# Queries and keys of two heads from seven block products instead of eight, in the QKV block of a transformer kernel

## The chip, the cores and the metric

The kernel runs on one core of one Trainium2 chip. A core has TensorE (PE: matmuls, and PEld, the loading of their weights), VectorE (DVE), ScalarE (ACT), GpSimd (POOL) and SyncE (SP, which here only issues DMAs). They run side by side, each through its own list of instructions in a fixed order, and wait for one another by semaphores that the code sets by hand. The metric is the time of one execution on the device, in microseconds (us), as the median of several runs.

## The reference, cut to what matters

x is 1024 tokens of 512 numbers in fp32; the kernel computes six residual layers, of which the change touches the second:

```python
x = x + 0.5 * ffn(layernorm(x), ...)
x = x + attn(layernorm(x), Wq, bq, Wk, bk, Wv, bv, Wo, bo, gq, gk)   # 32 heads of 128
x = x + 0.5 * ffn(layernorm(x), ...)
x = x + 0.5 * ternary_ffn(x, ...)
x = x + retrieval_attn(layernorm(x), ...)
x = x + 0.5 * ternary_ffn(x, ...)

def attn(h, ...):
    q = rms_norm(h @ Wq + bq, gq)     # over all 4096 numbers of a token
    k = rms_norm(h @ Wk + bk, gk)
    v = h @ Wv + bv
    # softmax(q k^T / sqrt(128)) v, head by head, then @ Wo + bo
```

## The kernel before

Stages: a feed-forward layer to 93 us, the layer norm's tail to 101, **the QKV block from 101.4 to 638.4**, attention to 1740, then the rest. Matmuls are made in pairs of parts: each fp32 operand is split into a high part (fp32r, written by ACT) and a low part, the rest (by DVE, or POOL), and a product is high x high + high x low + low x high, three matmuls of 128x128 by 128x512 for every 128 of the 512 inputs (`product`, printed as L402 in the profile). So one unit, a tile of 128 outputs by 512 tokens, is 4 x 3 = 12 matmuls into one bank of PSUM.

The QKV block works in eight groups of four heads (`groups`: the first and last are written out, those between are a loop). A group has three phases, Q, K and V, of eight units each (u // 2 is the head, u % 2 the half of the tokens; for V a unit is 128 tokens by four heads). Its 1 MB of weights for a phase is loaded as one tile, split by ACT in one instruction (L734, 128x2048) and by DVE in one (`split`, L767), a whole phase before PE needs it. Per unit: DVE evicts the bank with the bias added (L826, or L824 for V) into one of four `res` tiles; for a query ACT writes the high part scaled with the gain (L752) and DVE the low part (`q_low`, L801), which SP stores to a scratch tensor in DRAM; keys and values are stored from `res` as they are. For the later RMS norm ACT squares every query and key tile (L755, `sq`, two buffers) and POOL adds the square to an accumulator (L865). In the first group POOL also adds the output bias to x (L855, eight times).

PE's only waits in the loop are for the phase's low weights (`w_lo_done`) and for the bank of four units ago (`res_done`). `ln_xT_hi`/`ln_xT_lo` are the two parts of x^T, normalised and transposed. The layer norm writes them at the end of the feed-forward stage, a 128-token tile at a time (L326 on ACT: high part; DVE: low part), and PE computes the first two units of the first phase, the queries, between its transposes.

## Time and profile before

| | |
|---|---|
| median of 3 runs | 2321.61 us (2321.32 to 2323.63) |
| the profiled execution's own time | 2324.25 us |
| its span | 2322.5 us |
| mean granted clock of TensorE in it | 0.989 |
| PE busy | 2256.0 us, 97% of the span |
| DVE busy | 1609.4 us, 69% |
| ACT busy | 1135.6 us, 49% |
| POOL busy | 828.8 us, 36% |

Rows of groups read: line of the code, engine, operation, output<-inputs, partitions x elements and types, x count, then busy us and mean ns of one, then idle time of the engine before them and what ended it. Rows of a timeline read: start us, duration us, engine, line, operation, output<-inputs; in brackets the idle time before it and who ended it. Durations of matmuls overlap, so the distance of two starts is what one costs; in a run of one instruction on DVE or ACT the next also starts slightly before the reported end of the last. Tile names are those of the program's buffers, some of which serve several purposes.

### The profile page before, as it was taken

The numbers are of one execution on the slowest core, as the hardware profiler recorded it, in microseconds if no ns is written. First come the engines' busy times: TensorE is split into PE (matmuls) and PEld (weight loads), VectorE is DVE, ScalarE is ACT, GpSimd is POOL, SyncE is SP. The second block draws the span as 40 slices with busy tenths as digits, with TensorE's granted clock in tenths as the row PEclk, the third lists the DMA queues.
The fourth block names the chain that finished last, engine by engine and source line by source line (L and its number), as shares of the span: only waits on it lengthen the run. The fifth ranks groups of instructions, "written<-read, shape, count | busy, mean of one in ns | idle before, by whom it ended". The sixth has DMA issues, their size and how long they took to land. (4 is left out here: it accounts for less than half of the span.)

```text
span 2322.5 us, 34366 instructions
## 1 busy us (share of the span) xinstructions
PE 2256.0 (97%) x11044; PEld 1874.1 (81%) x11044; DVE 1609.4 (69%) x2654; ACT 1135.6 (49%) x1845; POOL 828.8 (36%) x736
## 2 busy tenths in 40 slices
PE   7899999999989999999999999999998999899998
PEld 5688888888778888888888888888886788687887
DVE  5544444444378888888888888888886665785765
ACT  3233332322266666666666666666663344352442
POOL 4553332233222222212212222222214466672565
PEclk9999999999999999999999999999999999999999
DMA  3155555455332211211221221221201111141210
GB/s 114 47 181 191 190 177 183 168 187 184 132 107 71 81 55 67 81 66 56 81 72 50 81 72 50 81 78 44 81 24 41 51 68 44 33 129 37 73 59 37
DMA packets 106182, 210.47 MB, mean 91 GB/s; under 512 B 9728, under 2 KB 42496, under 8 KB 102784
## 3 DMA queue, kind: packets, MB, share of 16 engines
q1 hardware_dynamic: 106112, 209.57, 26.9%
q8 instruction: 39, 0.64, 0.1%
q14 instruction: 31, 0.25, 0.0%
HBM read 140.33 MB, written 69.21 MB: 90 GB/s over the span
## 5 line engine op out<-in xcount | busy, mean ns | idle before, releaser
L1106 ACT ACTIVATE at_pT_hi<-ps 128x512 fp32r<-128x512 f32 x512 | 278.3, 595 | 352.3 <-PE ps L1210 352.2
L1148 DVE TENSOR_REDUCE at_small<-ps 128x1 f32<-128x1024 f32 x256 | 312.5, 1221 | 84.0 <-PE ps L402 83.0
L1158 DVE TENSOR_TENSOR at_pT_lo<-ps,at_pT_hi 128x512 fp32r<-128x512 f32 x512 | 327.1, 680 | 3.8 <-ACT at_pT_hi L1106 3.8
L1113 ACT ACTIVATE at_probs<-ps,at_small,cols 128x1024 f32<-128x1024 f32 x256 | 309.2, 1208 | 28.2 <-DVE at_small L1150 21.6
L865 POOL TENSOR_TENSOR qkv_acc<-qkv_acc,qkv_sq 128x512 f32<-128x512 f32 x128 | 166.2, 1299 | 320.1 <-ACT qkv_sq L755 316.5
L1210 PEld LDWEIGHTS ps<-ident,at_probs 128*128 128x128 f32 x2048 | 239.2, 140 | 37.9 <-issue 4.4
L1210 PE MATMUL ps<-ident,at_probs 128*128 128x128 f32 x2048 | 266.4, 273 | 3.2 <-DVE at_pT_lo L1158 3.2
L1172 DVE SCALAR_TENSOR_TENSOR x<-ps,at_small,x 128x512 f32<-128x512 f32 x256 | 192.0, 750 | 10.2 <-PE ps L402 3.1
L1043 POOL TENSOR_TENSOR at_o_lo<-at_o_raw,at_o_hi 128x512 fp32r<-128x512 f32 x32 | 41.2, 1288 | 439.8 <-ACT at_o_hi L1127 439.8
L402 PE MATMUL ps<-ln_xT_hi,ln_xT_lo 128*128 128x512 f32 x768 | 196.0, 390 | 0.0
L826 DVE TENSOR_SCALAR qkv_res<-ps,cols 128x512 f32<-128x512 f32 x128 | 94.9, 748 | 141.7 <-PE ps L402 122.7
L1235 PE MATMUL ps<-at_pT_hi,ln_xT_lo 128*128 128x512 f32 x512 | 180.6, 393 | 0.7 <-DVE at_y_lo L1144 0.7
L402 PEld LDWEIGHTS ps<-ln_xT_hi,ln_xT_lo 128*128 128x128 f32 x768 | 144.2, 188 | 30.7
L402 PE MATMUL ps<-ln_xT_hi,q_hi 128*128 128x512 f32 x480 | 148.0, 390 | 0.0
L752 ACT ACTIVATE qkv_q_hi<-qkv_res,cols 128x512 fp32r<-128x512 f32 x64 | 46.3, 723 | 194.6 <-DVE qkv_res L826 194.6
L755 ACT ACTIVATE qkv_sq<-qkv_res 128x512 f32<-128x512 f32 x128 | 80.0, 625 | 121.3 <-DVE qkv_res L826 104.8
L402 PE MATMUL ps<-at_o_hi,at_y_hi 128*128 128x512 f32 x256 | 122.0, 477 | 3.9 <-DVE x L1172 3.5
L402 PE MATMUL ps<-ln_xT_hi,first_hi 128*128 128x512 f32 x280 | 113.3, 405 | 7.1 <-DVE ln_xT_lo L282 4.0
L1043 POOL TENSOR_TENSOR ln_xT_hi<-kn,ln_xT_hi 128x1024 fp32r<-128x1024 f32 x31 | 74.2, 2393 | 116.0 <-ACT ln_xT_hi L1083 116.0
L1235 PEld LDWEIGHTS ps<-at_pT_hi,ln_xT_lo 128*128 128x128 f32 x512 | 96.0, 188 | 22.1 <-issue 0.9
L824 DVE TENSOR_TENSOR qkv_res<-ps,qkv_bv 128x512 f32<-128x512 f32 x64 | 43.5, 688 | 98.9 <-PE ps L402 98.8
L402 PE MATMUL ps<-ln_xT_hi,first_lo 128*128 128x512 f32 x280 | 111.1, 397 | 0.0
(273 smaller groups left out, 5636.4 us busy)
## 6 DMA issues: line engine op xcount, KB each, us to landing
scratch_q_hi<-qkv_q_hi SPq DMA_DIRECT2D x64, 256.0 KB, 2.1
scratch_q_lo<-qkv_q_lo SPq DMA_DIRECT2D x64, 256.0 KB, 2.3
scratch_k<-qkv_res SPq DMA_DIRECT2D x64, 256.0 KB, 2.8
scratch_v<-qkv_res SPq DMA_DIRECT2D x64, 256.0 KB, 2.3
k_raw<-scratch_k SPq DMA_DIRECT2D x32, 512.0 KB, 3.8
at_v_raw<-scratch_v SPq DMA_DIRECT2D x32, 512.0 KB, 3.3
wq_raw<-in_Wq SPq DMA_DIRECT2D x8, 1024.0 KB, 6.5
qkv_w<-in_Wk SPq DMA_DIRECT2D x8, 1024.0 KB, 5.0
```

The source lines that it names most:

```text
L402: last = nc.tensor.matmul(out, s, m, start=(start and n == 0), stop=(stop and n == len(terms) - 1))
L755: nc.scalar.activation(sq[:, u % 2, :], res[u % 4][:], ACT.Square).then_inc(sq_done, 1)
L826: nc.vector.tensor_scalar(res[u % 4][:], core.bank(u % 4), bias[t][:, bass.ds(g * GROUP + u // 2, 1)], None, ALU.add)\
L865: nc.gpsimd.tensor_tensor(part, part, sq[:, u % 2, :], ALU.add).then_inc(acc_done, 1)
L1043: nc.gpsimd.tensor_tensor(dst, a, b, ALU.subtract).then_inc(done, 1)
L1106: nc.scalar.activation(pT2[jp][0][:, 4 * b:4 * b + 4, w * P:(w + 1) * P], T_BANKS[:, b * HALF:(b + 1) * HALF].rearrange("p (k n) -> p k n" ...
L1113: nc.scalar.activation(probs[l % 4][:], scores(l)[:], ACT.Exp, bias=nbias[:, l % 4:l % 4 + 1], scale=rq[:, l % NT:l % NT + 1], accum_out=s ...
L1148: nc.vector.reduce_max(maxes[:, l % 4:l % 4 + 1], scores(l)[:], AX.X).then_inc(s_max, 1)
L1158: nc.vector.tensor_tensor(pT2[jp][1][out], T_BANKS[:, b * HALF:(b + 1) * HALF].rearrange("p (k n) -> p k n", k=4), pT2[jp][0][out], ALU.su ...
L1172: nc.vector.scalar_tensor_tensor(out=x[:, tile, :], in0=core.bank(WO_BANK), scalar=rsums[:, c:c + 1], in1=x[:, tile, :], op0=ALU.mult, op1 ...
L1210: last = nc.tensor.transpose(T_BANKS[:, k * P:(k + 1) * P], probs[(l - T_LAG) % 4][:, k * P:(k + 1) * P], core.ident[:])
L1235: last = nc.tensor.matmul(core.bank(PV_BANK), a[:, k, :], b[:, k, :], start=(c == 0 and n == 0), stop=(c == 3 and n == len(terms) - 1))
```

## The change

Queries and keys are no longer made unit by unit, but in **quads**: one quad is the queries, or the keys, of two heads, that is four units (two heads by two halves of the tokens, 512 each), as a 2x2 block product of the weights' blocks A11, A12, A21, A22 (inputs 0 to 255 or 256 to 511 by head 1 or 2) and the blocks of x^T B11, B12, B21, B22. A group has four quads: j = 0 queries, 1 keys, 2 queries, 3 keys, and c = 4g + j counts them. The 2x2 product is made in the form of Strassen and Winograd, from seven products P1 to P7 of six matmuls each in place of eight, with four sums of weight blocks S1 to S4 per quad, four sums T1 to T4 of x^T made once, and sums of products:

```
P1 = A11 B11   P2 = A12 B21   P3 = S4 B22   P4 = A22 T4   P5 = S1 T1   P6 = S2 T2   P7 = S3 T3
U2 = P1 + P6   U3 = U2 + P7
C11 = P1 + P2   C21 = U3 + P4   C22 = U3 + P5   C12 = U2 + P5 + P3
```

P1, P6, P7 and P4 are added up in one PSUM bank (`e_bank`), which is read after each of the first three: `keep_p1` (ACT, into a tile printed as rk), `keep_u2` (DVE, qkv_u), `keep_u3` (ACT, qkv_u). P5 and P3 share a second bank, P2 has a third. The weight sums are made by POOL (`sums_of_weights`), their high parts by ACT (`high`, instructions of 512, 768, 256 and 256 columns), their low parts by DVE (`low`, the same sizes), a quad ahead of their use; C21 is evicted by ACT, the other three by DVE. P4 and P3 of quad j-1 are issued after P1 of quad j.

The rest: the weights of a quad are loaded as 512 KB; the value weights are split in four pieces of 128x512, two in step 0 and two in step 2 of the next group, instead of in one; the eight units of values of a group stand after its four quads, with P4 and P3 of quad 3 behind the first; in the first group six of the eight units come first, of which two lie between the transposes of the layer norm, where two query units lay; the layer norm also keeps x^T in fp32 (two ACT copies of 128x2x128 per tile), from which DVE makes T1 to T4 (four instructions of 128x2x512), ACT their high parts and DVE and POOL two low parts each.

The diff, cut to its core:

```diff
+        if self.keep is not None:
+            for t in [k - 4] if k < self.STEPS - 1 else [NT - 2, NT - 1]:
+                if t >= 0:
+                    act.wait_ge(self.s_lo, t + 1)
+                    for i, part in enumerate(self.keep):
+                        last = self.nc.scalar.activation(part[:, :, t * P:(t + 1) * P],
+                                                         self._psum(t)[:, 2 * i:2 * i + 2, :], ACT.Copy)
+                    last.then_inc(self.s_kept, 1)
...
-            wait(pe, self.s_lo, t - 1)
+            wait(pe, self.s_lo if self.keep is None else self.s_kept, t - 1)
...
+            def sums_of_weights(g, j):
+                c, w = g * QUADS + j, raw[j % 2]
+                s = [s_raw[:, i, :].rearrange("p (k c) -> p k c", k=2) for i in range(4)]
+                a11, a12, a21, a22 = w[:, 0:2, 0, :], w[:, 2:4, 0, :], w[:, 0:2, 1, :], w[:, 2:4, 1, :]
+                pool.wait_ge(w_in[j % 2], nth(g, j) * 16 + 16)
+                wait(pool, late_lo, c)
+                nc.gpsimd.tensor_tensor(s[0], a21, a22, ALU.add).then_inc(s_made, 1)
+                nc.gpsimd.tensor_tensor(s[2], a11, a21, ALU.subtract).then_inc(s_made, 1)
+                pool.wait_ge(s_made, c * 4 + 1)
+                nc.gpsimd.tensor_tensor(s[1], s[0], a11, ALU.subtract).then_inc(s_made, 1)
+                pool.wait_ge(s_made, c * 4 + 3)
+                nc.gpsimd.tensor_tensor(s[3], a12, s[1], ALU.subtract).then_inc(s_made, 1)
+            def add_square(g, j, kind):
+                m = (g * QUADS + j) * 4 + kind
+                pool.wait_ge(sq_done, m + 1)
+                pool.wait_ge(acc_done, m + 2)
+                part = acc[j % 2][:, half(kind) * HALF:(half(kind) + 1) * HALF]
+                nc.gpsimd.tensor_tensor(part, part, sq[:, kind % 2, :], ALU.add).then_inc(acc_done, 1)
...
+                for j in range(QUADS):
+                    if j + 1 < QUADS:
+                        sums_of_weights(g, j + 1)
+                    if j > 0:
+                        for kind in (C22, C21, C12):
+                            add_square(g, j - 1, kind)
+                    add_square(g, j, C11)
+                    if is_first(g):
+                        add_output_bias(j)
+                if not is_last(g):
+                    sums_of_weights(g + 1, 0)
+                for kind in (C22, C21, C12):
+                    add_square(g, QUADS - 1, kind)
+                if is_last(g):
...
+            def high(g, j):
+                c, w, o = g * QUADS + j, raw[j % 2], left_hi[j % 2]
+                act.wait_ge(w_in[j % 2], nth(g, j) * 16 + 16)
+                wait(act, p7_done, c - 1)
+                nc.scalar.activation(o[:, 0:2 * PART].rearrange("p (k c) -> p k c", k=KB), w[:, :, 0, :], ACT.Copy)\
+                    .then_inc(left_hi_done, 1)
+                act.wait_ge(s_made, c * 4 + 3)
+                nc.scalar.activation(o[:, S1 * PART:(S3 + 1) * PART].rearrange("p (s n) -> p s n", s=3),
+                                     s_raw[:, 0:3, :], ACT.Copy).then_inc(left_hi_done, 1)
+                wait(act, p3_done, c - 1)
+                nc.scalar.activation(o[:, A22 * PART:(A22 + 1) * PART].rearrange("p (k c) -> p k c", k=2),
+                                     w[:, 2:4, 1, :], ACT.Copy).then_inc(left_hi_done, 1)
+                act.wait_ge(s_made, c * 4 + 4)
+                nc.scalar.activation(o[:, S4 * PART:(S4 + 1) * PART], s_raw[:, 3, :], ACT.Copy)\
+                    .then_inc(left_hi_done, 1)
+            def shared(g, j, kind):
+                n, m = nth(g, j), (g * QUADS + j) * 4 + kind
+                act.wait_ge(c_done[kind], g * QUADS + j + 1)
+                if is_query(j):
+                    wait(act, q_stored[kind], n * 32)
+                    nc.scalar.activation(q_hi[kind][:], res[kind][:], ACT.Copy,
+                                         scale=gain_now[:, head(j, kind):head(j, kind) + 1]).then_inc(q_hi_done, 1)
+                wait(act, acc_done, m + 1)
+                nc.scalar.activation(sq[:, kind % 2, :], res[kind][:], ACT.Square).then_inc(sq_done, 1)
...
+            def keep_p1(g, j):
+                c = g * QUADS + j
+                act.wait_ge(p1_done, c + 1)
+                wait(act, c_done[C11], c)
+                nc.scalar.activation(p1, e_bank(j), ACT.Identity, bias=bias(j, C11)).then_inc(p1_kept, 1)
+            def keep_u3(g, j):
+                c = g * QUADS + j
+                act.wait_ge(p7_done, c + 1)
+                wait(act, c_done[C22], c)
+                nc.scalar.activation(u3, e_bank(j), ACT.Identity, bias=bias(j, C22)).then_inc(u3_kept, 1)
+            def evict21(g, j):
+                c = g * QUADS + j
+                act.wait_ge(p4_done, c + 1)
+                res_free(act, g, j, C21)
+                nc.scalar.activation(res[C21][:], e_bank(j), ACT.Identity, bias=bias(j, C21)).then_inc(c_done[C21], 1)
...
+                act.wait_ge(now_done, g + 1)
+                for j in range(QUADS):
+                    keep_p1(g, j)
+                    if j > 0:
+                        shared(g, j - 1, C22)
+                        evict21(g, j - 1)
+                        shared(g, j - 1, C21)
+                        shared(g, j - 1, C12)
+                    if j + 1 < QUADS:
+                        high(g, j + 1)
+                    if not is_first(g) and is_query(j):
+                        split_values(g, j)
+                        split_values(g, j + 1)
+                    shared(g, j, C11)
+                    keep_u3(g, j)
+                shared(g, QUADS - 1, C22)
+                evict21(g, QUADS - 1)
+                shared(g, QUADS - 1, C21)
+                shared(g, QUADS - 1, C12)
+                if not is_last(g):
+                    high(g + 1, 0)
 
             groups(act, body)
...
+            def low(g, j):
+                c, w, hi, lo = g * QUADS + j, raw[j % 2], left_hi[j % 2], left_lo[j % 2]
+                def piece(n, a, b, src, k):
+                    v.wait_ge(left_hi_done, c * 4 + n)
+                    return nc.vector.tensor_tensor(lo[:, a * PART:b * PART].rearrange("p (k n) -> p k n", k=k), src,
+                                                   hi[:, a * PART:b * PART].rearrange("p (k n) -> p k n", k=k),
+                                                   ALU.subtract)
+                wait(v, p7_done, c - 1)
+                piece(1, A11, S1, w[:, :, 0, :], KB)
+                piece(2, S1, A22, s_raw[:, 0:3, :], 3).then_inc(early_lo, 1)
+                wait(v, p3_done, c - 1)
+                piece(3, A22, S4, w[:, 2:4, 1, :], 2)
+                piece(4, S4, 7, s_raw[:, 3:4, :], 1).then_inc(late_lo, 1)
...
+            def evict(g, j, kind, bank, kept):
+                res_free(v, g, j, kind)
+                nc.vector.tensor_tensor(res[kind][:], bank, kept, ALU.add).then_inc(c_done[kind], 1)
+            def evict11(g, j):
+                c = g * QUADS + j
+                v.wait_ge(p2_done, c + 1)
+                v.wait_ge(p1_kept, c + 1)
+                evict(g, j, C11, A_BANK, p1)
+            def evict22(g, j):
+                c = g * QUADS + j
+                v.wait_ge(p5_done, c + 1)
+                v.wait_ge(u3_kept, c + 1)
+                evict(g, j, C22, d_bank(j), u3)
+            def keep_u2(g, j):
+                c = g * QUADS + j
+                v.wait_ge(p6_done, c + 1)
+                wait(v, c_done[C12], c)
+                nc.vector.tensor_scalar(u2, e_bank(j), bias_now[j % 2][:, head(j, C12):head(j, C12) + 1], None,
+                                        ALU.add).then_inc(u2_kept, 1)
...
+                for j in range(QUADS):
+                    if j > 0:
+                        evict22(g, j - 1)
+                        q_low(g, j - 1, C11)
+                        q_low(g, j - 1, C22)
+                        evict12(g, j - 1)
+                    keep_u2(g, j)
+                    if j > 0:
+                        q_low(g, j - 1, C21)
+                    if j + 1 < QUADS:
+                        low(g, j + 1)
+                    if j > 0:
+                        q_low(g, j - 1, C12)
+                    if not is_first(g) and is_query(j):
+                        split_values(g, j)
+                        split_values(g, j + 1)
+                    evict11(g, j)
+                evict22(g, QUADS - 1)
+                evict_values(g, units[0])
+                evict12(g, QUADS - 1)
+                if not is_last(g):
+                    v.wait_ge(c_done[C21], g * QUADS + QUADS)
+                    next_columns(g + 1)
+                    low(g + 1, 0)
+                for u in units[1:]:
+                    evict_values(g, u)
...
+            def times(out, j, part, right, more=False):
+                return product(nc, out, [(left(j, part, k), right[k]) for k in range(2)], start=not more, more=more)
+            def fourth(g, j):
+                c = g * QUADS + j
+                pe.wait_ge(u3_kept, c + 1)
+                pe.wait_ge(late_lo, c + 1)
+                times(e_bank(j), j, A22, T4, more=True).then_inc(p4_done, 1)
+            def third(g, j):
+                c = g * QUADS + j
+                pe.wait_ge(c_done[C22], c + 1)
+                times(d_bank(j), j, S4, B22, more=True).then_inc(p3_done, 1)
+            def second(g, j):
+                wait(pe, c_done[C11], g * QUADS + j)
+                times(A_BANK, j, A12, B21).then_inc(p2_done, 1)
...
+            def body(g):
+                for j in range(QUADS):
+                    c = g * QUADS + j
+                    pe.wait_ge(early_lo, c + 1)
+                    wait(pe, c_done[C21], c - 1)
+                    times(e_bank(j), j, A11, B11).then_inc(p1_done, 1)
+                    if j > 0:
+                        fourth(g, j - 1)
+                        third(g, j - 1)
+                    else:
+                        second(g, j)
+                    pe.wait_ge(p1_kept, c + 1)
+                    times(e_bank(j), j, S2, T2, more=True).then_inc(p6_done, 1)
+                    if j > 0:
+                        second(g, j)
+                    wait(pe, c_done[C12], c - 1)
+                    times(d_bank(j), j, S1, T1).then_inc(p5_done, 1)
+                    pe.wait_ge(u2_kept, c + 1)
+                    times(e_bank(j), j, S3, T3, more=True).then_inc(p7_done, 1)
+                for u in tail_units(g):
+                    values_unit(g, u)
+                    if u == tail_units(g)[0]:
+                        fourth(g, QUADS - 1)
+                        third(g, QUADS - 1)
```

**ScalarE, inside a group.** Before, at the end of a Q phase and in the K phase (qkv_w, wq: weight tiles):

```order
L752 ACTIVATE qkv_q_hi<-qkv_res,cols 128x512
L755 ACTIVATE qkv_sq<-qkv_res 128x512
L734 ACTIVATE qkv_w_hi<-qkv_w 128x2048
L755 ACTIVATE qkv_sq<-qkv_res 128x512 x8
L734 ACTIVATE wq_hi<-wq_raw 128x2048
```

After, step j = 1 of the first group, from `keep_p1(1)` to `keep_u3(1)` (ln_xn is the buffer of the squares, qkv_left_hi the high parts of quads 0 and 2, first_raw their weights, qkv_s_raw the sums):

```order
L930 ACTIVATE rk<-ps,cols 128x512
L918 ACTIVATE qkv_q_hi<-qkv_res,cols 128x512
L921 ACTIVATE ln_xn<-qkv_res 128x512
L942 ACTIVATE qkv_res<-ps,cols 128x512
L918 ACTIVATE qkv_q_hi<-qkv_res,cols 128x512
L921 ACTIVATE ln_xn<-qkv_res 128x512
L918 ACTIVATE qkv_q_hi<-qkv_res,cols 128x512
L921 ACTIVATE ln_xn<-qkv_res 128x512
L899 ACTIVATE qkv_left_hi<-first_raw 128x512
L902 ACTIVATE qkv_left_hi<-qkv_s_raw 128x768
L905 ACTIVATE qkv_left_hi<-first_raw 128x256
L908 ACTIVATE qkv_left_hi<-qkv_s_raw 128x256
```

Behind these stand the square of C11 (L921) and `keep_u3(1)` (L936). The one split of a phase became four pieces inside every step, between the copies that PE waits for.

**VectorE, inside a group.** Before, at the end of a Q phase and in the K phase:

```order
L826 TENSOR_SCALAR qkv_res<-ps,cols 128x512
L801 SCALAR_TENSOR_TENSOR qkv_q_lo<-qkv_res,cols,qkv_q_hi 128x512
L767 TENSOR_TENSOR qkv_w_lo<-qkv_w,qkv_w_hi 128x2048
L826 TENSOR_SCALAR qkv_res<-ps,cols 128x512
L801 SCALAR_TENSOR_TENSOR qkv_q_lo<-qkv_res,cols,qkv_q_hi 128x512
L826 TENSOR_SCALAR qkv_res<-ps,cols 128x512 x7
```

After, step j = 1 of the first group (L1016 evicts C22, C12 of quad 0 and last C11 of quad 1, L1040 is `keep_u2(1)`, L992 `low(2)`):

```order
L1016 TENSOR_TENSOR qkv_res<-ps,qkv_u 128x512
L1009 SCALAR_TENSOR_TENSOR qkv_q_lo<-qkv_res,cols,qkv_q_hi 128x512 x2
L1016 TENSOR_TENSOR qkv_res<-ps,qkv_u 128x512
L1040 TENSOR_SCALAR qkv_u<-ps,cols 128x512
L1009 SCALAR_TENSOR_TENSOR qkv_q_lo<-qkv_res,cols,qkv_q_hi 128x512
L992 TENSOR_TENSOR qkv_left_lo<-first_raw,qkv_left_hi 128x512
L992 TENSOR_TENSOR qkv_left_lo<-qkv_s_raw,qkv_left_hi 128x768
L992 TENSOR_TENSOR qkv_left_lo<-first_raw,qkv_left_hi 128x256
L992 TENSOR_TENSOR qkv_left_lo<-qkv_s_raw,qkv_left_hi 128x256
L1009 SCALAR_TENSOR_TENSOR qkv_q_lo<-qkv_res,cols,qkv_q_hi 128x512
L1016 TENSOR_TENSOR qkv_res<-ps,rk 128x512
```

The four low parts now stand between `keep_u2(1)` and the eviction of C11 of the same quad.

**GpSimd, the first group.** Before:

```order
L850 MEMSET qkv_acc 128x1024 x2
L855 TENSOR_TENSOR x<-x,qkv_bo 128x512 x8
L865 TENSOR_TENSOR qkv_acc<-qkv_acc,qkv_sq 128x512 x16
```

After, one step (second_raw is the weights of quads 1 and 3, acc the accumulator, rk the output bias here):

```order
L840 TENSOR_TENSOR qkv_s_raw<-second_raw 128x256
L841 TENSOR_TENSOR qkv_s_raw<-second_raw 128x256
L843 TENSOR_TENSOR qkv_s_raw<-qkv_s_raw,second_raw 128x256
L845 TENSOR_TENSOR qkv_s_raw<-second_raw,qkv_s_raw 128x256
L852 TENSOR_TENSOR acc<-acc,ln_xn 128x512 x4
L856 TENSOR_TENSOR x<-x,rk 128x512
```

Four weight sums came in ahead of every four additions.

## Rows read from the trace of the kernel before

**Rows 1.** The page's first part: busy time, share of the span, instructions, by engine

```profile
PE 2256.0 (97%) x11044; PEld 1874.1 (81%) x11044; DVE 1609.4 (69%) x2654; ACT 1135.6 (49%) x1845; POOL 828.8 (36%) x736
```

**Rows 2.** Window of a group: busy us (instructions) of PE, PEld, DVE, ACT, POOL; clock, DMA, GB/s

```profile
222.00:287.00 65.00, 65.00 (x289) 53.82 (x288) 29.40 (x37) 20.29 (x27) 20.63 (x16) 1.00 0.55 182
```

**Rows 3.** Timeline, PE at a unit's end, and the eviction of that unit

```profile
225.75 0.39 PE L402 MATMUL ps<-qkv_w_hi,ln_xT_lo 128*128 128x512 f32 x1
...
226.27 0.69 DVE L824 TENSOR_TENSOR qkv_res<-ps,qkv_bv 128x512 f32<-128x512 f32 x1 [2.03 <-PE ps L402]
```

**Rows 4.** Timeline, DVE and ACT near the block's start, and DVE in a later group

```profile
110.52 3.00 DVE L767 TENSOR_TENSOR qkv_w_lo<-qkv_w,qkv_w_hi 128x2048 fp32r<-128x2048 f32 x1 [5.39 <-ACT qkv_w_hi L734]
113.44 1.40 DVE L826 TENSOR_SCALAR qkv_res<-ps,cols 128x512 f32<-128x512 f32 x2
...
117.02 1.11 DVE L801 SCALAR_TENSOR_TENSOR qkv_q_lo<-qkv_res,cols,qkv_q_hi 128x512 fp32r<-128x512 f32 x1
...
114.22 0.72 ACT L752 ACTIVATE qkv_q_hi<-qkv_res,cols 128x512 fp32r<-128x512 f32 x1 [3.72 <-DVE qkv_res L826]
114.84 0.61 ACT L755 ACTIVATE qkv_sq<-qkv_res 128x512 f32<-128x512 f32 x1
115.36 0.70 ACT L752 ACTIVATE qkv_q_hi<-qkv_res,cols 128x512 fp32r<-128x512 f32 x1
...
197.50 2.29 DVE L767 TENSOR_TENSOR qkv_w_lo<-qkv_w,qkv_w_hi 128x2048 fp32r<-128x2048 f32 x1 [2.46 <-ACT qkv_w_hi L734]
199.71 0.75 DVE L826 TENSOR_SCALAR qkv_res<-ps,cols 128x512 f32<-128x512 f32 x1
200.37 0.74 DVE L801 SCALAR_TENSOR_TENSOR qkv_q_lo<-qkv_res,cols,qkv_q_hi 128x512 fp32r<-128x512 f32 x1
```

**Rows 5.** A group of instructions, 93 to 645 us: busy us, mean ns | idle before

```profile
L841 DVE TENSOR_TENSOR kn<-k_raw,rk 128x1024 f32<-128x1024 f32 x1 | 1.2, 1226 | 0.1
```

**Rows 6.** ACT, all of line 1620: min/median/max ns, first and last start

```profile
L1620 ACT ACTIVATE rt_r<-ps,ln_small x16: 667/670/673, 2025.1 to 2095.6; 128x512 f32<-128x512 f32 x16
```

**Rows 7.** POOL: a timeline at 201 us, and groups or lines of its additions

```profile
201.36 4.04 POOL L865 TENSOR_TENSOR qkv_acc<-qkv_acc,qkv_sq 128x512 f32<-128x512 f32 x3 [4.24 <-ACT qkv_sq L755]
...
L865 POOL TENSOR_TENSOR qkv_acc<-qkv_acc,qkv_sq 128x512 f32<-128x512 f32 x128 | 166.2, 1299 | 320.1 <-ACT qkv_sq L755 316.5
L855 POOL TENSOR_TENSOR x<-x,qkv_bo 128x512 f32<-128x512 f32 x8 | 13.4, 1704 | 6.3 <-DMA qkv_bo<-in_bo 6.3
...
L1048 POOL TENSOR_TENSOR kn<-k_raw,rk x31: 2382/2409/2420, 647.3 to 1668.9; 128x1024 f32<-128x1024 f32 x31
```

**Rows 8.** DVE line 1678, the retrieval stage's low parts beside POOL

```profile
L1678 DVE TENSOR_TENSOR rt_wo_lo<-rt_wo,rt_wo_hi x8: 679/1364/1367, 2039.4 to 2111.1; 128x512 fp32r<-128x512 f32 x8
```

**Rows 9.** PE after two waits elsewhere (timeline), and windows behind them, columns as rows 2

```profile
640.23 0.47 PE L402 MATMUL ps<-first_hi,q_hi 128*128 128x512 f32 x1 [1.87 <-PEq L624]
640.54 0.39 PE L402 MATMUL ps<-first_lo,q_hi 128*128 128x512 f32 x1
...
2111.81 0.50 PE L402 MATMUL ps<-rt_wo_hi,rt_ret_hi 128*128 128x512 f32 x1 [2.06 <-DVE rt_wo_lo L1678]
...
641.00:650.00 9.00, 6.40 (x30) 4.53 (x28) 4.44 (x8) 4.29 (x7) 2.69 (x2) 1.00 0.78 262
2113.00:2117.00 4.00, 4.00 (x14) 3.09 (x13) 1.67 (x3) 2.32 (x3) 0.72 (x1) 0.57 0.00 0
```

**Rows 10.** The block's start on PE, and two loads (KB, us to landing)

```profile
114.24 0.80 PE L402 MATMUL ps<-ln_xT_hi,wq_hi 128*128 128x512 f32 x1 [6.94 <-DVE qkv_res L826]
...
115.26 0.63 PE L402 MATMUL ps<-ln_xT_hi,wq_lo 128*128 128x512 f32 x1
115.68 0.63 PE L402 MATMUL ps<-ln_xT_hi,wq_hi 128*128 128x512 f32 x1
...
qkv_w<-in_Wk SPq DMA_DIRECT2D x8, 1024.0 KB, 5.0
qkv_bv<-in_bv SPq DMA_DIRECT2D x8, 256.0 KB, 5.5
```

495 lines of the change are left out of this document (288 added, 207 removed).

## The prediction

> **What bounds the kernel now.** I read the page first. TensorE (PE) is busy for 2,256.0 of 2,322.5 us, VectorE (DVE) for 69% of it, ScalarE (ACT) for 49%, GpSimd (POOL) for 36% [rows 1]: PE sets the end. Then the window of one of the eight groups of heads, the block that changes. In 65.0 us PE is busy for 65.00 us and starts 289 matmuls, at full clock, so 288 distances: one starts every 0.226 us (0.2267 over the whole block). A group (3 projections x 8 units x 12 = 288 matmuls) takes 65.3 us. DVE has 29.4 us of work there, ACT 20.3, POOL 20.6 [rows 2]. There is no wait to win inside a group: the change can gain only by fewer matmuls, and loses where PE begins to wait for the other three.
>
> **What is removed.** A quad (queries or keys of two heads) takes seven products of six matmuls, 42, in place of 48. Four quads a group: 24 matmuls x 0.2267 us = 5.44 us a group, 192 matmuls and 43.5 us in all. Nothing else runs on PE in those slots, so all of it counts.
>
> **What is added on PE's path.** Before, PE waited only for a PSUM bank freed long ago. Now four products of a quad go into one bank, which is read in between: P1 is kept (ACT), P6 is added and the sum kept (DVE, `keep_u2`), P7 is added and kept (ACT, `keep_u3`), and P4 is added only then. Between P6(j) and P4(j) PE has work of its own: P6, P5, P7 and P1(j+1) for j = 0, which is 24 x 0.2267 = 5.44 us; P2 lies there too for j = 1 and 2, 6.80 us; for j = 3 a unit of values as well. Against that stands a chain which the order on the two engines fixes: `keep_u2(j)`, one low part of a query (where j-1 is a query), the four low parts of the next quad's weights, another query low part or the two low parts of value weights, `evict11(j)` on DVE; then on ACT the high part (of a query), the square, and `keep_u3(j)`. The durations:
> - a unit's last matmul starts at 225.75 and its eviction at 226.27, 0.52 later [rows 3]; from the start of P6 to `keep_u2` are five spacings, 0.52 and 0.05 for the semaphore (113.44 + 0.75 to 114.22 [rows 4]): 1.70 us.
> - PSUM evictions on DVE last 0.75 (with a bias column) and 0.69 (with a second operand), a query low part 0.74 [rows 3, 4], and the next starts some 0.09 before the reported end: 0.66, 0.60, 0.65.
> - a subtraction of two SBUF tiles lasts 1.23 us for 1,024 columns and 2.29 for 2,048 [rows 4, 5]: 1.04 per 1,024 and 0.16 fixed. The four low parts (512, 768, 256, 256 columns) follow one another in 0.61 + 0.88 + 0.35 + 0.35 = 2.19 us; two value low parts in 1.22.
> - ACT: after a square the next starts 0.52 later, after a query high part of 0.72 it is 0.62 [rows 4]; an eviction lasts 0.67 [rows 6], and I take 0.69 for `keep_u3`, which adds a bias column.
>
> Two more hand-overs are 0.10. For j = 0 the chain is 1.70 + 0.66 + 2.19 + 1.22 + 0.69 + 0.62 + 0.52 + 0.69 + 0.10 = 8.39 us against 5.44: PE waits 2.95. For j = 1 (a key: no high part; two query low parts): 1.70 + 0.66 + 0.65 + 2.19 + 0.65 + 0.69 + 0.52 + 0.69 + 0.10 = 7.85 against 6.80: 1.05. For j = 2: 8.39 against 6.80: 1.59. For j = 3 no weights stand in between: none. Together 5.59 us a group, already more than the 5.44 gained; over eight groups 44.7, less 2.4 in group 0, which has no value splits in these steps. **Bare: -43.5 + 44.7 - 2.4 = -1.2 us.**
>
> **What lengthens the chain.** POOL: a step gives it four sums of 128x256 and four squares of 128x512. Squares follow 1.35 us apart (4.04 for three; mean 1.30 alone), 1,024 columns take 2.41 [rows 7], so 256 columns take some 0.74, 0.79 with its semaphore. The ACT square of unit m waits until POOL has added m-2, and POOL has the next quad's four sums (3.1 us) ahead of three of its additions. Followed through, instruction by instruction, ACT's last square before the next high parts comes 1.24 us later than DVE is ready for it at j = 2, and 0.24 at j = 1: 1.5 us a group.
> Contention: two-input DVE work on SBUF is slower while POOL works. Beside POOL's `x += bo` (mean 1,704 ns against 1,299 for the same size) a low part of 2,048 took 3.00 us instead of 2.29, a query low part 1.11 instead of 0.74; the retrieval stage's 512-column low part took 0.68 at least, 1.36 in the middle [rows 4, 7, 8]. That is 0.36 us for each POOL instruction met, if the long one met two. Some five are met inside the three chains: 1.8 us a group. Bounds: 0, and twice that (the 1.36 row: 0.68 each). I take the first because it comes from this block's own instructions.
> A matmul after a wait is followed 0.31 us later, not 0.23 [rows 9]: 0.08 for each of some four waits, 0.3. Sum 3.6 a group, **+28.8 us**; bounds +2.6 (restarts only) and +43.
> The Trainium skill, "SBUF — State Buffer", section "Who interferes with whom", says that a DVE instruction with two SBUF inputs contends with a GpSimd instruction that reads SBUF and that the shared ports are an exclusive lock. If that meant one whole POOL instruction for each meeting, it would be nearer the 0.68; the 3.00 us row speaks for a part of one.
>
> **Clock.** A wait of 2.06 us was followed by a stretch at a granted clock of 0.57, one of 1.87 by 1.00 [rows 9]; 0.57 over 4 us is some 1.7 us lost. After the 6.94 us wait at 114.24 they start 0.43 apart [rows 10]: the lower of the two levels, 1.2 GHz. The waits at j = 0 and 2 (above 3 with contention and POOL's order) are longer than the 2.06 that was followed by a fall, that at j = 1 is shorter than the 1.87 that was not. Eight would be 13.6 us, sixteen 27, none 0; six falls, **+10 us**, because PE stays busy between the waits here more than in the retrieval stage.
>
> **Start and layer norm.** Before, the block starts with the 6.94 us wait for the value weights and a slow stretch of some 5 us behind it, matmuls 0.43 apart [rows 10]. After, values come first, from four pieces, and the first quad waits for the four sums of x^T (two-input subtractions of 1,024 columns, 1.23 each), for their low parts (two on POOL, 2.4 each) and for POOL's weight sums behind them; the bias of the values lands 5.5 us after its issue [rows 10]. I see waits of 2 to 4 and of some 3.5 us in place of 6.94 and the slow stretch: 0, bounds -5 and +6. In the layer norm's tail ACT makes two more copies per tile, which the next transposes wait for: **+1**, bounds 0 and 3 (256 columns are half of the 0.61 of 512 [rows 4]: two copies more for each of eight tiles, of which I count the last ones, where PE has little else). The end of the block changes little: the last values are still stored last; 0, bounds -2 and +3. On SP's queue the load for quad j+2 now stands ahead of the stores of quad j-1, and waits for the low parts of quad j; these are made a step earlier, so neither is held up, and 512 KB have a whole quad, 9.5 us, to land, where 1,024 KB land in 5.0 us [rows 10]: nothing.
>
> **Sum:** -1.2 + 28.8 + 10 + 1 = +38.6 against the profiled execution's own 2,324.25, so 2,362.9; that execution lay 2.6 above the median of its runs, 2,321.61, so I forecast a median of **2,360 us**.
>
> **Rivals.**
> A, the saving stays (faster). Mechanism: DVE and ACT finish their chain within PE's own work, so P4 never waits. For it: all three engines have spare time over a group (DVE 29.4 of 65.0). Against it: spare time doesn't help in a fixed order of which each piece waits for P6. Every us off the chain counts in three steps of eight groups, 24 us; the kernel becomes faster from a chain some 1.8 us shorter than with all additions above. Hidden but for 0.5 us a group: -43.5 + 4 + 1 gives 2,283. 8%.
> B, the bare chain is right, POOL costs little and the clock stays up: -1.2 + 2.6 + 1 gives 2,324, with the 1.5 us of POOL's order a group 2,336; from 2,318 to 2,340. For it: no row shows 256-column POOL work beside DVE. 15%.
> C, contention as in the 1.36 us row (1.6 a group more, +12.8) and a fall of the clock at both long waits (+17): 2,390, from 2,382 to 2,405. 17%. With the contention alone, the lock of the skill's page, it is 2,373, inside my main case.
> Main case, 2,340 to 2,382: 60%.
>
> **How the numbers follow.** The forecast is the main case's. 80% lie in 2,330 to 2,398: it leaves out A (8%), half of B and the far end of C. About 0.2%, 4.6 us, is what a measurement of this kernel can tell from no change. Faster by more: A and the fastest of B, 9%. Within it: the bare sum with nothing on top, 5%. Slower: 86%.
>
> **What would show it.** In the profile after: 10,852 matmuls; a window of one group some 69 us long in place of 65.3, and 70 with its fall of the clock; PE waits before P4 of quads 0, 1 and 2 released by `keep_u3`, some 3.2, 1.5 and 3.4 us with contention and POOL's order, none of quad 3; the low parts of 512 columns 0.69 us alone and about 1.05 beside POOL; ACT idle before a square on account of POOL's additions once or twice a group; granted clock below 1 after the j = 0 wait in most groups. Groups of 65 us or less would prove me wrong at the chain; waits of the right number but of 1 to 2 us, at the contention and POOL terms; full clock throughout, at the clock term. A first quad that waits for 10 us would be the start.

## The result, and the profile after

The changed kernel takes 2382.74 us (median of 4 runs, 2381.41 to 2382.99), against 2322.62 for the kernel before: 1.0252 times as long, 95% interval 1.0236 to 1.0268. The forecast was slower, at 2,360 us in a range of 2,330 to 2,398; 57 to 60 us were lost, where 38.6 had been added up. The profiled execution took 2381.41 us, span 2379.6, 57.16 us above the one of before. (Ahead of the forecast the kernel before had three runs, median 2321.61; a fourth, of 2329.48, moved the median to 2322.62.)

The page's first part, columns as in [rows 1]; TensorE has 192 matmuls less and is busy for 13 us less, all others have more:

```profile
PE 2242.9 (94%) x10852; PEld 1846.5 (78%) x10852; DVE 1686.6 (71%) x2794; ACT 1236.0 (52%) x2094; POOL 936.8 (39%) x865
```

The window of about one group, columns as in [rows 2]; and below it four microseconds behind or around the end of each of three waits of group 3 (groups are counted from 0):

```profile
300.00:372.00 72.00, 62.86 (x266) 50.30 (x265) 39.04 (x53) 32.11 (x57) 34.83 (x33) 0.98 0.50 165
336.00:340.00 4.00, 4.00 (x19) 3.29 (x19) 3.39 (x5) 3.40 (x6) 3.92 (x5) 1.00 0.57 166
348.00:352.00 4.00, 3.84 (x17) 3.18 (x18) 1.38 (x2) 2.65 (x5) 3.92 (x6) 1.00 0.82 291
362.00:366.00 4.00, 4.00 (x14) 3.11 (x14) 1.90 (x4) 2.64 (x6) 1.67 (x2) 0.70 0.53 160
```

266 matmuls now take 72 us, where 288 took 65.3. The timeline of TensorE's waits in that group (P4 of quad 0; P1 of quad 2, P4 of quad 1; P1 of quad 3, P4 of quad 2), and the same wait for P4 of quad 0 one group on:

```profile
334.79 0.50 PE L417 MATMUL ps<-qkv_right_hi,qkv_left_hi 128*128 128x512 f32 x1 [2.63 <-ACT qkv_u L936]
...
344.91 0.50 PE L417 MATMUL ps<-ln_xT_hi,qkv_left_hi 128*128 128x512 f32 x1 [1.68 <-DVE qkv_left_lo L992]
348.16 0.50 PE L417 MATMUL ps<-qkv_right_hi,queries 128*128 128x512 f32 x1 [1.60 <-ACT qkv_u L936]
357.12 0.50 PE L417 MATMUL ps<-ln_xT_hi,queries 128*128 128x512 f32 x1 [0.50 <-DVE first_parts L992]
361.53 0.79 PE L417 MATMUL ps<-qkv_right_hi,qkv_left_hi 128*128 128x512 f32 x1 [2.73 <-ACT qkv_u L936]
362.12 0.63 PE L417 MATMUL ps<-qkv_right_lo,qkv_left_hi 128*128 128x512 f32 x1
362.55 0.63 PE L417 MATMUL ps<-qkv_right_hi,qkv_left_lo 128*128 128x512 f32 x1
...
406.62 0.50 PE L417 MATMUL ps<-qkv_right_hi,qkv_left_hi 128*128 128x512 f32 x1 [2.63 <-ACT qkv_u L936]
```

The reader is to see three things. `keep_u3` (L936) releases three of the five waits, low parts (L992) the two others. A group takes 406.62 - 334.79 = 71.8 us. And the first 2.63 us wait is followed by matmuls at full clock (granted clock 1.00), the 2.73 us one by matmuls 0.43 apart (0.70 in its four microseconds), the lower level, called half clock below.

Why P1 of quad 2 waits is seen on the three other engines just before (timeline of step 1; DVE, ACT, POOL):

```profile
339.20 0.75 DVE L1040 TENSOR_SCALAR qkv_u<-ps,cols 128x512 f32<-128x512 f32 x1 [0.61 <-PE ps L417]
339.87 1.34 DVE L1009 SCALAR_TENSOR_TENSOR qkv_q_lo<-qkv_res,cols,qkv_q_hi 128x512 fp32r<-128x512 f32 x1
341.87 1.04 DVE L992 TENSOR_TENSOR qkv_left_lo<-first_raw,qkv_left_hi 128x512 fp32r<-128x512 f32 x1 [0.67 <-ACT qkv_left_hi L899]
342.84 2.02 DVE L992 TENSOR_TENSOR qkv_left_lo<-qkv_s_raw,qkv_left_hi 128x768 fp32r<-128x768 f32 x1
...
340.69 0.63 ACT L921 ACTIVATE ln_xn<-qkv_res 128x512 f32<-128x512 f32 x1 [1.26 <-POOL acc L852]
341.23 0.61 ACT L899 ACTIVATE qkv_left_hi<-first_raw 128x512 fp32r<-128x512 f32 x1
...
334.32 1.28 POOL L852 TENSOR_TENSOR acc<-acc,ln_xn 128x512 f32<-128x512 f32 x1 [21.05 <-ACT ln_xn L921]
335.55 0.73 POOL L840 TENSOR_TENSOR qkv_s_raw<-first_raw 128x256 f32<-128x256 f32 x1
...
339.36 4.68 POOL L852 TENSOR_TENSOR acc<-acc,ln_xn 128x512 f32<-128x512 f32 x3
```

POOL waits 21.05 us for a square, then makes four sums before its three additions; ScalarE waits for the additions with a square; its high part (L899), and with it DVE's low part, comes behind (DVE idles 0.67 us). The low part of 768 columns then takes 2.02 us; alone it is 0.955 (below). What made it longer is POOL's third addition, seen singly (timeline):

```profile
342.44 1.60 POOL L852 TENSOR_TENSOR acc<-acc,ln_xn 128x512 f32<-128x512 f32 x1
```

It runs to 344.04. The low part starts at 342.84, 1.20 us before that, and lasts 1.07 us longer than alone: it stands until the addition has ended, but for some 0.14 us. The addition in turn had started inside the low part of 512 columns (to 342.91) and lasts 0.31 us longer than alone. This holds throughout: in the loop (185 to 610 us) of the changed kernel 168 instructions of DVE have two SBUF inputs. 58 began while a POOL instruction ran and took as much longer as that one still had to run, less 0.14 us, each within 0.06 us (0.59 on average); the other 110 lasted as alone. Of POOL's 192 instructions there, 43 began inside such a DVE instruction and were longer by its rest, again less 0.14, each within 0.03 us; the other 149 lasted as alone. So a meeting has no fixed price: whoever comes second waits for the rest of the first.

The block from its first matmul behind the layer norm to attention's first takes 538.6 us before and 593.7 after; attention and all behind it are as long as before (1682.2 and 1682.1). The same count for every run, in us, from its profiled execution ("half clock" is what matmuls 0.43 apart cost over 0.2267 each, good to about 1 us). The profiled execution is one of the runs and not always near the median: no_pool's took 2342.3 us, u3_first's 2344.6, spread_start_c11's 2315.3.

| | median of runs | ratio to before | block | PE's waits | half clock |
|---|---|---|---|---|---|
| before | 2322.6 | | 538.6 | 9.7 | 5.1 |
| after | 2382.7 | 1.0252 | 593.7 | 79.0 | 22.4 |
| no_pool | 2334.7 | 1.0039 | 553.3 | 45.1 | 21.0 |
| no_squares_added | 2352.7 | 1.0109 | 565.7 | 51.2 | 26.3 |
| no_weight_sums | 2343.7 | 1.0096 | 553.4 | 56.5 | 7.5 |
| p1_repeated | 2370.9 | 1.0199 | 583.2 | 30.9 | 6.1 |
| c11_before_values | 2355.1 | 1.0132 | 564.9 | 64.8 | 8.5 |
| u3_first | 2348.9 | 1.0107 | 555.8 | 47.5 | 19.2 |
| sums_early_only | 2349.8 | 1.0115 | 561.8 | 64.3 | 7.9 |
| u3_first_sums_early | 2322.2 | 0.9992 | 532.2 | 34.0 | 10.1 |
| u3_sums_values_spread | 2319.7 | 0.9982 | 529.1 | 31.7 | 9.0 |
| spread_start_sums | 2316.6 | 0.9968 | 528.5 | 32.1 | 7.5 |
| spread_start_c11 | 2319.6 | 0.9978 | 527.0 | 29.6 | 8.8 |

### The profile page after: what moved, and what is told of

Its sections match the earlier page's. It is cut to its first block and busy times, and to the rows that moved or that the text cites. A ratio compares the mean times of both kernels' runs of the same rounds, so it can differ in the third digit from the quotient of the medians.

```text
span 2379.6 us, 34723 instructions
## 1 busy us (share of the span) xinstructions
PE 2242.9 (94%) x10852; PEld 1846.5 (78%) x10852; DVE 1686.6 (71%) x2794; ACT 1236.0 (52%) x2094; POOL 936.8 (39%) x865
## 5 line engine op out<-in xcount | busy, mean ns | idle before, releaser
L852 POOL TENSOR_TENSOR acc<-acc,ln_xn 128x512 f32<-128x512 f32 x128 | 177.3, 1385 | 255.0 <-ACT ln_xn L921 250.2
L417 PE MATMUL ps<-ln_xT_hi,queries 128*128 128x512 f32 x816 | 222.2, 392 | 8.2 <-DVE first_parts L992 8.2
L417 PE MATMUL ps<-ln_xT_hi,first_parts 128*128 128x512 f32 x656 | 221.4, 399 | 7.0 <-DVE ln_xT_lo L288 4.0
L417 PEld LDWEIGHTS ps<-ln_xT_hi,queries 128*128 128x128 f32 x816 | 153.2, 188 | 44.3 <-DVE first_parts L992 12.0
L417 PEld LDWEIGHTS ps<-ln_xT_hi,first_parts 128*128 128x128 f32 x656 | 125.5, 191 | 35.8 <-issue 4.8
L921 ACT ACTIVATE ln_xn<-qkv_res 128x512 f32<-128x512 f32 x128 | 79.9, 624 | 96.2 <-DVE qkv_res L1016 71.0
L1016 DVE TENSOR_TENSOR qkv_res<-ps,qkv_u 128x512 f32<-128x512 f32 x64 | 44.2, 691 | 111.7 <-ACT qkv_u L936 47.1
L1374 POOL TENSOR_TENSOR ln_xT_hi<-keys,ln_xT_hi 128x1024 fp32r<-128x1024 f32 x31 | 74.1, 2390 | 116.1 <-ACT ln_xT_hi L1414 116.1
L417 PE MATMUL ps<-ln_xT_lo,first_parts 128*128 128x512 f32 x280 | 110.7, 395 | 0.0
```

The costliest lines, as they stand in the source:

```text
L417: last = nc.tensor.matmul(out, s, m, start=(start and n == 0), stop=(stop and n == len(terms) - 1), skip_group_check=more)
L852: nc.gpsimd.tensor_tensor(part, part, sq[:, kind % 2, :], ALU.add).then_inc(acc_done, 1)
L921: nc.scalar.activation(sq[:, kind % 2, :], res[kind][:], ACT.Square).then_inc(sq_done, 1)
L1016: nc.vector.tensor_tensor(res[kind][:], bank, kept, ALU.add).then_inc(c_done[kind], 1)
L1374: nc.gpsimd.tensor_tensor(dst, a, b, ALU.subtract).then_inc(done, 1)
```

## The experiments

**The chain without POOL (no_pool).**

```diff
+                if not (is_first(g) and j == 0):
+                    return
...
-                nc.gpsimd.tensor_tensor(part, part, sq[:, kind % 2, :], ALU.add).then_inc(acc_done, 1)
+                pass
...
-                act.wait_ge(s_made, c * 4 + 3)
+                act.wait_ge(s_made, 3)
...
-                wait(act, acc_done, m + 1)
```

The first two lines stand in `sums_of_weights`, the next two in `add_square`; ScalarE no longer waits for either.

> POOL's additions of squares and all its sums of weights but those of the very first quad are left out (queries and keys are not computed rightly), with ScalarE's waits for them; PE, DVE and ScalarE do the same work as in the changed kernel. This is the bare chain of the prediction: waits before P4 of quads 0, 1 and 2 of 2.95, 1.05 and 1.6 us, 5.6 a group, none before P1, so 8 x 3.5 us less than the changed kernel and some of the half clock: 2345 to 2356. Rival: the durations of the bare chain were too short or too long and POOL costs less or more than 3.5 us a group: waits off 5.6 by more than 1.

The timeline of PE's waits in one group (P4 of quads 1, 2 and, a group on, 0); then groups of DVE's instructions from 180 to 610 us (busy us, mean ns | idle before), one of this run and two of the changed kernel:

```profile
331.25 0.50 PE L417 MATMUL ps<-qkv_right_hi,queries 128*128 128x512 f32 x1 [0.71 <-ACT qkv_u L934]
342.38 0.50 PE L417 MATMUL ps<-qkv_right_hi,qkv_left_hi 128*128 128x512 f32 x1 [1.31 <-ACT qkv_u L934]
...
386.10 0.79 PE L417 MATMUL ps<-qkv_right_hi,qkv_left_hi 128*128 128x512 f32 x1 [2.63 <-ACT qkv_u L934]
```

```profile
L990 DVE TENSOR_TENSOR qkv_left_lo<-qkv_s_raw,qkv_left_hi 128x768 fp32r<-128x768 f32 x13 | 12.4, 955 | 0.3
```

```profile
L992 DVE TENSOR_TENSOR qkv_left_lo<-qkv_s_raw,qkv_left_hi 128x768 fp32r<-128x768 f32 x12 | 19.5, 1623 | 0.2
L1009 DVE SCALAR_TENSOR_TENSOR qkv_q_lo<-qkv_res,cols,qkv_q_hi 128x512 fp32r<-128x512 f32 x48 | 49.9, 1059 | 0.8
```

A wait in the trace is 0.16 us shorter than the gap that the prediction reckons in (a matmul is shown for 0.39 us where its slot is 0.2267). So the gaps are 2.79, 0.87 and 1.47, 5.13 a group, against 2.95, 1.05 and 1.59, 5.6 in all: the bare chain was right to 0.2 us at each place. The rival, an error above 1 us, is out. POOL then costs 9.15 + 0.8 - 5.13 = 4.8 us in group 3 of the changed kernel, not 3.3 (4.3 on average over groups 1 to 7, since the wait before P1 of quad 2 is only 0.3 to 0.6 us in groups whose first wait is followed by half clock). The time, 2334.7, was lower than the 2345 to 2356 expected and spread widely, 2325.6 to 2342.3 (the clock, below).

**One half of POOL's work at a time (no_squares_added, no_weight_sums).** The first leaves out the additions only, the second the sums only, by the same lines as above.

> POOL's additions of the squares are left out (the accumulators stay at zero, so the RMS norm of queries and keys is not computed rightly), and ScalarE's squares no longer wait for them; POOL's sums of weights stay. Theory (POOL's order 1.5 us a group and contention 1.8 us): waits before P1 of quads 2 and 3 go, those before P4 go to 3.4, 1.1 and 2.1: 9.1 -> 6.6 us a group, the time 2358 to 2368 with the clock's stretches left. Low parts of 768 columns 0.95 us as when alone. Rival: POOL's work doesn't matter, the fixed order of DVE and ScalarE alone makes 9 us: 2378 to 2385.

> POOL's sums of weights are left out after the first quad (queries and keys not computed rightly), its additions of squares stay. With the run without the additions and the run without both this splits POOL's part. Theory: waits before P4 of 2.6 to 3.0, 1.1 to 1.6 and 1.6 to 2.1, none before P1: 6.5 us a group, 2350 to 2362. Rival: the additions alone hold up the squares and with them the high parts: a wait before P1 of quad 2 of over 1 us stays, 2365 or more.

Without the additions the waits of a group are 3.17, 0.71 and 1.85, 5.7 us, and the 768-column low part takes 956 ns on average: the sums alone overlap no low part and cost 1.1 us a group over no_pool's 4.65. Without the sums they are 2.63, 0.19, 1.59 and 2.14, 6.55 us (6.5 expected): the additions alone cost 1.9. Both together cost 4.5 us (9.15 - 4.65). The rest, 1.5, neither has alone: the sums put off additions for which ScalarE waits, and the 768-column low part then falls beside an addition (1,623 ns on average, 945 without the sums). In the chains of a group DVE's instructions are longer than alone by nothing without the additions, by 2.0 us without the sums and by 3.0 with both, so some 1.0 of the 1.5 is slower DVE work and the rest waiting in order. Both times were some 5 to 6 us below the range given; for no_weight_sums the waits were as expected.

**Is it the place of keep_u3? (u3_first).**

```diff
-                    shared(g, j, C11)
                     keep_u3(g, j)
+                    shared(g, j, C11)
```

> ScalarE issues keep_u3(j) before the high part and square of C11(j), in every step; nothing else changes. Theory: the three waits of PE before P4 (2.63, 1.60 and 2.74 us a group in the changed kernel) exist because keep_u3 stands behind evict11 and so behind all low parts; they should shrink below 0.5 us each. The low parts are still late, so what comes last next is P1 of quads 2 and 3, now 1.7 and 0.5 us, which should grow to some 3.3 and 2.5. Waits 9.1 -> 6 to 6.5 us a group, a group of 68 to 69.5 us instead of 71.9 to 73, the time 2355 to 2365. Rival: the place of keep_u3 doesn't matter, the low parts and POOL bound the loop at 9 us of waits: 2378 to 2385.

PE's waits in a group are now two, for low parts (timeline):

```profile
335.62 0.50 PE L417 MATMUL ps<-ln_xT_hi,qkv_left_hi 128*128 128x512 f32 x1 [3.89 <-DVE qkv_left_lo L992]
347.83 0.50 PE L417 MATMUL ps<-ln_xT_hi,queries 128*128 128x512 f32 x1 [0.78 <-DVE first_parts L992]
```

The three waits for `keep_u3`, 51.5 us in the changed kernel, are gone, and part of them came back before P1 of quad 2, as 3.9 us: 9.15 -> 4.7 a group, a gain of 33.9 us in the time from one exchanged pair of lines. The time, 2348.9, is below the 2355 to 2365 expected: the wait before P1 of quad 3 did not grow as expected (0.8, not 2.5). The rival, no effect of the place, is out.

**Are the value low parts in the chain? (c11_before_values).**

```diff
+                    evict11(g, j)
                     if not is_first(g) and is_query(j):
                         split_values(g, j)
                         split_values(g, j + 1)
-                    evict11(g, j)
```

> The changed kernel with one thing moved: on VectorE the eviction of C11 stands ahead of the two low parts of value weights in steps 0 and 2, not behind them; keep_u3 and all else as in the changed kernel. Theory (the chain of the prediction, in which these two low parts are 1.22 us): the waits before P4 of quads 0 and 2 fall by 1.2 us each, 2.63 -> 1.4 and 2.74 -> 1.5, the others stay; 8 x 2.4 = 17 to 19 us less, and since no wait is then above 1.7 us the half clock goes too, another 10 to 17: 2346 to 2356. Rival 1: the clock falls all the same, 2362 to 2366. Rival 2: the value low parts are not in the chain that PE waits for (it is ScalarE's or POOL's): no change, 2378 to 2384.

The waits before P4 of quads 0 and 2 fell to 1.43 and 1.53, by the 1.20 that two low parts cost in the sum (1.22); the others stayed at 1.67, 1.59 and 0.49. The time came to 2355.1, of which 14 us are half clock that is gone. Rivals 1 and 2 are out.

**Does the half clock come from the waits? (p1_repeated).**

```diff
+                    for _ in range([0, 2, 1, 2][j]):
+                        times(e_bank(j), j, A11, B11)
                     times(e_bank(j), j, A11, B11).then_inc(p1_done, 1)
```

> PE makes P1 of quads 1 and 3 three times and of quad 2 twice (each time from the start, so the bank holds the same), 30 matmuls more a group, 6.8 us, put just ahead of P4, where PE waits 2.6, 1.6 and 2.7 us. PE's work rises by 54 us in all, and the waits should be filled: below 0.3 us before each P4. Clock theory: the stretches at half clock follow these waits and go with them, so although PE does more, the time falls by some 1.5 to 2.5 us a group: 2362 to 2372. Rival: the stretches at half clock come from something else (the wait alone costs): granted clock as before and the time the same or longer, 2382 to 2390.

The window as for the changed kernel, and then what is left before P4 (timeline):

```profile
300.00:372.00 72.00, 69.59 (x303) 56.00 (x302) 39.49 (x54) 32.52 (x57) 36.00 (x35) 1.00 0.51 171
```

```profile
345.31 0.50 PE L417 MATMUL ps<-qkv_right_hi,queries 128*128 128x512 f32 x1 [0.24 <-ACT qkv_u L936]
```

With 240 matmuls (54 us) more, the kernel is 11.9 us faster than the changed one. The idle time went from 79.0 to 30.9 us, the half clock from 22.4 to 6.1, about what it was before the change: what half clock the change brought goes with the waits. (One such stretch stands behind none of them: ten matmuls from 616.75 us before and thirteen from 675.80 after, some 24 us or more behind the last wait and right behind the 128x1 matmuls that sum up the squares.)

**POOL's order alone, and with keep_u3 (sums_early_only, u3_first_sums_early).**

```diff
-                    if j + 1 < QUADS:
-                        sums_of_weights(g, j + 1)
                     if j > 0:
                         for kind in (C22, C21, C12):
                             add_square(g, j - 1, kind)
+                    if j + 2 < QUADS:
+                        sums_of_weights(g, j + 2)
+                    elif j == QUADS - 1 and not is_last(g):
+                        sums_of_weights(g + 1, 0)
                     add_square(g, j, C11)
...
```

> Only POOL's sums are a step earlier; keep_u3 stays behind C11's high part and square. Theory: POOL's order (1.5 us a group in the prediction) goes: the waits before P1 of quads 2 and 3 vanish, those before P4 stay at 2.6 to 3.4, 1.1 to 1.6 and 2.1, some 7 us a group in place of 9.1, with the half clock as before: 2362 to 2370. The order on ScalarE and POOL's order together are then worth more than the sum of each alone, if the run with both comes to 2318 or less: 34 us for keep_u3 alone, some 16 for the sums alone, and 65 or more together. Rival: both act on the same wait, and the gains are no more than added: both together 2333 or more.

> The run with keep_u3 ahead of C11's square, and besides POOL makes the weight sums of a quad one addition and one step earlier: behind the three additions of quad j-1 it makes the sums of quad j+2 and only then adds C11(j)'s square, so POOL uses the time in which it waited for that square. The work is the same. Theory: the 3.9 us wait before P1 of quad 2 and most of the late low parts came from high parts that stood behind squares that stood behind POOL's additions and sums; waits of 0.8 (P3 of quad 0), 1.1 (P1 of quad 2) and 0.6 us are left, a group takes 63.3 to 64.5 us, less than the 65.3 of the kernel before, hardly any half clock is left (all waits under 1.9 us), and the time is 2306 to 2318: faster than before by 0.2 to 0.7%. Rival: the low parts themselves, with contention, make 3 us or more before P1 of quad 2 wherever the sums stand: 2335 to 2350.

The sums alone take 14.7 us of waits (16 expected), and the time falls by 32.9, to 2349.8, not the 2362 to 2370 expected: the half clock fell from 22.4 to 7.9, though the wait before P4 of quad 0 grew to 3.18 us. Together with `keep_u3` first the time is 2322.2, as before the change (0.9984 to 1.0001), not the 2306 to 2318 expected. The claim that both are worth more than their sum is wrong: 60.5 us together, 33.9 and 32.9 alone; in waits 45.0 against 31.5 + 14.7. What is left in a group (timeline):

```profile
312.03 0.50 PE L417 MATMUL ps<-ln_xT_hi,qkv_left_hi 128*128 128x512 f32 x1 [0.48 <-DVE qkv_res L1019]
320.93 0.50 PE L417 MATMUL ps<-ln_xT_hi,qkv_left_hi 128*128 128x512 f32 x1 [1.77 <-DVE qkv_left_lo L995]
331.65 0.50 PE L417 MATMUL ps<-ln_xT_hi,queries 128*128 128x512 f32 x1 [0.91 <-DVE first_parts L995]
```

Before P1 of quad 2 it is 1.77, not 1.1: with POOL's work packed closer, the low parts meet it again (768 columns 1.40 and 1.50 us on average, 0.955 alone). A group takes 64.3 us, 1.0 less than before the change, and the block 532.2, 6.4 less. Of this the profiled execution (2322.2 against 2324.25) loses 1.7 us in the layer norm and 2.7 behind the block, 1684.9 in place of 1682.2; why the part behind is longer is not shown. Between the versions it differs from 1681.6 to 1684.9, though its code is the same.

**A version that beats both (u3_sums_values_spread, spread_start_sums, spread_start_c11).** On top of that, the value splits one, one and two in steps 0, 1, 2; then quad 1's weight sums at the block's start ahead of POOL's low parts of T3 and T4; then C11 ahead of the value splits on DVE. The first two, in part:

```diff
+                    if not is_first(g):
+                        for k in ((0,), (1,), (2, 3), ())[j]:
+                            split_values(g, k)
...
                 pool.wait_ge(t_hi_done, 3 + i)
+                if i == 0:
+                    sums_of_weights(0, 1)
                 nc.gpsimd.tensor_tensor(t_lo[b], of_raw(k, h), t_hi[b], ALU.subtract).then_inc(t34_lo, 1)
```

> The same, and the four splits of value weights stand in steps 0, 1 and 2 (one, one, two) in place of two in step 0 and two in step 2. Theory: the 0.8 us wait before P3 of quad 0, whose C22 is evicted behind two value low parts, goes; one of 0.7 before P3 of quad 1 comes; a group takes 62.3 to 63.5 us, the time is 2300 to 2312. Rival: what is taken from step 0 is lost in step 1 in full: no difference from the run without the spread.

> The run with keep_u3 first, POOL's sums early and the values spread, and besides, at the block's start, POOL makes the weight sums of quad 1 ahead of its two low parts of T3 and T4 (3.2 and 2.4 us), not behind them and the clearing of the accumulators. Theory: the 2.7 us wait before P1 of quad 1 in the first group goes, as the sums are ready 5 us sooner, and the half clock behind it, and no new wait comes since T3 is needed 1 us later than it is made: 3 to 6 us less than the 2319.7 of the run without it, 2313.5 to 2317. Rival: P7 of quad 0 or P4 waits for T3's or T4's low part instead: no difference, 2318 to 2321.

> The same, and C11 evicted ahead of the value low parts on VectorE. Theory: with keep_u3 first nothing on PE waits for C11 any more, but ScalarE's square of C11 and with it POOL come 0.6 to 1.2 us sooner, against C22's eviction 0 us later: at most 0.3 us a group, 2311 to 2317. Rival: the order of the two is without effect, within 1 us of the run without it.

2319.7 us is 0.18% below before (0.9973 to 0.9990), 2316.6 is 0.32% below (0.9956 to 0.9980). The spread gave less than expected (2300 to 2312): a group shrank by only some 0.3 us. With the start changed the median is 3.0 us lower, inside the range expected, but not by the mechanism expected: before P1 of quad 1 the wait fell from 2.66 to 1.07, while the next one grew from 1.22 to 3.00, and PE's waits are 32.1 us in all, against 31.7. The block of the profiled execution is only 0.6 us shorter, the part behind it 2.1, so the gain is not shown to come from the edit. Moving C11 gave nothing that can be told (2319.6, range 2315.3 to 2322.2; 2311 to 2317 expected). The best version in its window: 301 matmuls in 72 us, and one wait of 1.93 us for low parts a group (in five of seven groups two short ones, 0.66 and 0.37, as well; window, then timeline):

```profile
300.00:372.00 72.00, 70.03 (x301) 57.09 (x300) 42.84 (x58) 34.62 (x62) 35.70 (x32) 0.98 0.56 182
```

```profile
319.63 0.78 PE L417 MATMUL ps<-ln_xT_hi,qkv_left_hi 128*128 128x512 f32 x1 [1.93 <-DVE qkv_left_lo L996]
```

## Why the prediction was right or wrong

The direction, the place and the mechanism held: PE waits for `keep_u3`, which stands behind C11's eviction, which stands behind the low parts, and the waits eat more than 24 matmuls a group are worth. The size was 18.6 us short: the time lies inside the range given but at the very end of the main case (2,382). The two profiled executions, term by term, with waits as gaps (0.16 added to each):

| term | predicted | measured |
|---|---|---|
| 192 matmuls less | -43.5 | -43.5 |
| gaps in groups 1 to 7 | 7 x 8.9 = 62.3 | 65.7 |
| gaps in group 0, to P1 of group 1 | 6.5 | 14.3 |
| the block's first wait | 0 (start) | 2.84 - 7.10 = -4.3 |
| slower first matmuls after waits | 2.6 | 5.2 (what is left; 42 waits more at 0.13 give 5.5) |
| half clock | 10 | 22.4 - 5.1 = 17.3 |
| layer norm | 1 | 103.84 - 101.60 = 2.2 |
| the block's end | 0 | 0.3 |
| sum | 38.9 | 57.2 |

(The 38.9 is the 38.6 of the prediction, with a rounding.)

- **The bare chain**: 5.6 a group predicted, 5.13 in the run without POOL. c11_before_values confirms its 1.22 term.
- **POOL**: 3.3 a group predicted (order 1.5, contention 1.8), 4.8 measured in group 3, 4.3 on average. The error of the bare chain hides half of this one in the sum, which is luck: 8.9 a group was said, 9.4 it is. The single waits differ from those named: 2.63 where some 3.2 was said, 1.68 + 1.60 where 1.5 was, 0.50 + 2.73 where 3.4 was. I had no wait before P1 at all. The step that was mis-sized is the price of contention, 0.36 us for each of some five POOL instructions met. In the chains of group 3 DVE's instructions are longer than alone by nothing at j = 0 (the wait before P4 of quad 0 is 2.63 with POOL and without it), by 0.59 + 0.36 + 1.07 at j = 1 and by 0.98 at j = 2: 3.0 us, from four meetings. The other 1.8 of the 4.8 is waiting in order, for which 1.5 had been said.
- **How the rows were misread**: the 0.36 came from the 3.00 us row [rows 4], "if the long one met two". It waited for one. The views of the kernel before that decide it, the two neighbours of that row on POOL, then the 1.36 us row of [rows 8] and what ran beside it:

```profile
110.11 1.26 POOL L855 TENSOR_TENSOR x<-x,qkv_bo 128x512 f32<-128x512 f32 x1 [6.33 <-DMA qkv_bo<-in_bo]
111.33 3.32 POOL L855 TENSOR_TENSOR x<-x,qkv_bo 128x512 f32<-128x512 f32 x1
...
2068.81 1.29 POOL L1592 TENSOR_TENSOR rt_sig_lo<-rt_sig,rt_sig_hi 128x512 fp32r<-128x512 f32 x1 [1.29 <-ACT rt_sig_hi L1630]
2069.28 1.36 DVE L1678 TENSOR_TENSOR rt_wo_lo<-rt_wo,rt_wo_hi 128x512 fp32r<-128x512 f32 x1 [0.62 <-ACT rt_wo_hi L1633]
```

The low part of 110.52 came 0.85 us before the first addition ended and is 0.71 longer than alone; the second addition came inside it and waited for it, 3.32 us in place of 1.3. The one of 2069.28 came 0.82 before the end and is 0.68 longer. The two prices of the prediction are one rule at two moments.
- The Trainium skill's rule ("SBUF — State Buffer", section "Who interferes with whom") holds here: two-input work of DVE on SBUF slows beside POOL (query low parts 745 ns without the additions, 1,059 with), PSUM evictions don't (691 ns with POOL's work and without). Its exclusive lock agrees with the trace too, if it is read as a wait for the rest of the instruction that came first, up to 1.09 us here, and not for a whole one at each meeting.
- **Clock**: six falls of 1.7 us were reckoned, a guess between 0 and 27, taken too near the low end; 17.3 us is what it cost, confirmed by p1_repeated (16.3 us less half clock with the waits filled). The falls came after 8 of the loop's 12 long waits, and not in most groups after the one at j = 0, as said, but after 3 of the 6 there and 5 of the 6 at j = 2.
- **Start**: "0" was the wrong sum of right parts. The first wait is 2.68 in place of 6.94, as said, but in group 0 follow waits of 3.02, 1.05, 0.94, 1.50, 1.70, 1.46 and then 3.58 before P1 of group 1; the prediction had one of 3.5. The timeline of the changed kernel at the first wait, at the 3.02 and at the last:

```profile
109.50 0.50 PE L417 MATMUL ps<-wv_hi,ln_xT_hi 128*128 128x512 f32 x1 [2.68 <-DVE v_res L1053]
...
127.93 0.50 PE L417 MATMUL ps<-ln_xT_hi,queries 128*128 128x512 f32 x1 [3.02 <-DVE first_parts L992]
...
179.31 0.49 PE L417 MATMUL ps<-ln_xT_hi,qkv_left_hi 128*128 128x512 f32 x1 [3.58 <-DVE qkv_left_lo L992]
```

- Rival C (contention of 0.68 and a fall at every long wait, 2,382 to 2,405) was nearer in its contention, 3.4 us a group against 1.8 in the main case and 3.0 measured. Its clock term, 10 + 17 us, was too high by more than the main case's was too low: measured 17.3. The time, 2,382.7, is on the line between the two. Rival A was what the change could have been: its 2,283 was reached by no version; 2316.6 is the best found, with 32 us of waits left.

## What to carry to other kernels

Fewer products help only as far as every intermediate is read and written in time: for each product that accumulates on a bank being read, add up the chain from the product before to the release, in the order of the engines' lists, and compare it with the matmuls in between. A copy for which TensorE waits belongs ahead of everything on its engine that nobody waits for; here one exchanged pair of lines gave back 34 us, and sums made in POOL's idle time 33. Where DVE work on two SBUF tiles can meet POOL work, price each meeting as the rest of the instruction that is running, so look at when it comes, not only how often. When waits of some two microseconds appear in a loop, reckon with the clock as well.

## What the runs showed of the hardware that was not expected

- A wait of 2 us or more is neither always nor never followed by half clock. In the loops (185 to 610 us) of the changed kernel 8 of 12 such waits were, within 1.7 us, in u3_first 7 of 7, in no_pool 5 of 6, in no_squares_added 4 of 6, in no_weight_sums 3 of 12, and in sums_early_only 2 of 13, although its longest waits are 3.18 us. Nor is 2 us a border: in no_squares_added all six waits of 1.85 us were followed by it, in u3_first_sums_early two of seven of 1.77, in spread_start_c11 four of seven of 1.84 to 1.96. In p1_repeated, whose longest waits there are 1.7 us, none was, and in c11_before_values neither. What decides stays open. The times spread with it: six runs of no_pool took 2325.6 to 2342.3, the two slowest at a mean granted clock of 0.983 and the others at 0.987 or 0.988, where the kernel before went from 2321.0 to 2327.9 on the same chip.
- POOL is slowed too, by the same rule: its additions take 1,385 ns on average in the changed kernel against 1,299 [rows 7], 256-column sums 0.74 us alone and 1.20 when they start inside one of DVE's query low parts.
- A wait costs PE some 0.3 us more than the idle time shown: 0.16 of the last matmul's slot and 0.13 because the next ones start 0.34 and 0.24 apart.
